# x laid out transposed as well and the mean folded into Wq, in a cross-attention + int8 FFN kernel on one core

## The reference, cut to what matters

```
x = x + xattn(layernorm(x), ctx, ctx, Wq, Wo)          # x: 4 x 2048 x 512, ctx: 4 x 77 x 512
    Q, K, V = split16(q @ Wq.T), split16(k @ Wq.T), split16(v @ Wq.T)
    attn    = softmax(Q K^T / sqrt(32)); out = (attn V) @ Wo.T
x = x + ffn(layernorm(x))                              # int8 fake quantisation of activations and weights
    h = quant(silu(xq @ wg.T) * (xq @ wu.T)); out = h @ quant(w_down).T       # inner size 1408
layernorm(x) = (x - mean) / sqrt(var + 1e-5)           # over the last axis, no scale or shift
```

## Time and profile before

| | |
|---|---|
| median of 3 runs | 1194.74 us (1194.72 to 1195.95) |
| profiled execution | 1194.37 us, of which the span is 1192.5 us |
| PE busy | 1125.9 us, 94% of the span |
| DVE, ACT, POOL busy | 861.6, 661.0 and 160.0 us |
| mean granted TensorE clock | 0.981 of 2.4 GHz |
| slots 3 to 24 (from 81.97 to 295.27 us) | 213.3 us for 22 slots |
| slots 25 to 55 (to 599.28 us) | 304.0 us for 31 slots |
| slots 56 to 65 (to 677.32 us) | 78.0 us for 10 slots |

### The profile page before, as it was taken

The page is one execution under the profiler, slowest core; times in us unless marked ns, Lnnn a source line. Parts: engine busy times, 40 slices in busy tenths (PEclk is TensorE's granted clock), DMA queues, the critical chain, the costliest instruction groups (busy, mean ns, idle before and its releaser), DMA issues. The chain is left out here.

```text
span 1192.5 us, 17719 instructions
## 1 busy us (share of the span) xinstructions
PE 1125.9 (94%) x6357; PEld 645.7 (54%) x6386; DVE 861.6 (72%) x1616; ACT 661.0 (55%) x819; POOL 160.0 (13%) x124
## 2 busy tenths in 40 slices
PE   5789999999999999999999969999999999799898
PEld 4555666666666666666665534444444444344333
DVE  5457888888878787877665667787777777575564
ACT  3347666556565655565544436657566663854450
POOL 1300000020000100000000000000000000357578
PEclk9989999999999999999999979999999999899999
DMA  5125555455343434332114626766767512899977
GB/s 182 36 59 141 125 133 132 130 130 135 103 130 108 125 109 124 109 106 65 63 54 151 216 79 229 257 219 236 237 223 251 175 46 89 333 412 419 422 279 257
DMA packets 130096, 203.51 MB, mean 171 GB/s; under 512 B 58080, under 2 KB 66912, under 8 KB 124128
## 3 DMA queue, kind: packets, MB, share of 16 engines
q1 hardware_dynamic: 130016, 202.46, 52.2%
HBM read 117.75 MB, written 72.48 MB: 160 GB/s over the span
## 5 line engine op out<-in xcount | busy, mean ns | idle before, releaser
L655 PE MATMUL a_Q<-a_xnT,wq 128*128 128x512 f32 x768 | 196.6, 405 | 3.1 <-DVE a_xnT L587 2.4
L1003 POOL TENSOR_TENSOR c_y<-x,c_y 128x512 f32<-128x512 f32 x64 | 114.3, 1816 | 554.7 <-DVE c_y L1037 544.1
L889 DVE SCALAR_TENSOR_TENSOR h<-e_U,x_gus,e_sg 128x512 f32<-128x512 f32 x176 | 131.9, 749 | 72.5 <-PE e_U L929 46.7
L834 ACT ACTIVATE e_sg<-e_G,x_gus 128x512 f32<-128x512 f32 x176 | 119.0, 685 | 117.0 <-PE e_G L925 117.0
L925 PE MATMUL e_G<-e_cT,gu 128*128 128x512 bf16 x689 | 179.3, 380 | 2.3 <-ACT e_cT L848 1.5
L929 PE MATMUL e_U<-e_cT,gu 128*128 128x512 bf16 x690 | 179.7, 380 | 0.7
L691 PE MATMUL a_O<-a_wo,a_aT 128*128 128x512 f32 x720 | 177.1, 395 | 0.0
L1075 PE MATMUL c_Y<-dn,gu 128*128 128x512 bf16 x704 | 158.4, 388 | 15.3 <-DVE gu L1030 15.3
L655 PEld LDWEIGHTS a_Q<-a_xnT,wq 128*128 128x128 f32 x768 | 142.2, 191 | 55.9 <-issue 26.4
L691 PEld LDWEIGHTS a_O<-a_wo,a_aT 128*128 128x128 f32 x720 | 133.4, 189 | 28.1 <-issue 2.5
L453 ACT ACTIVATE a_pr<-a_S 77x2048 f32<-77x2048 f32 x64 | 120.2, 1879 | 41.3 <-PE a_S L644 41.3
(11 more groups left out here) (134 smaller groups left out, 1354.2 us busy)
## 6 DMA issues: line engine op xcount, KB each, us to landing
x<-x_d SPq DMA_DIRECT2D x32, 1024.0 KB, 7.3
h_d<-h SPq DMA_DIRECT2D x24, 1024.0 KB, 4.1
h<-h_d SPq DMA_DIRECT2D x11, 1536.0 KB, 18.4
xa<-in_x SPq DMA_DIRECT2D x64, 256.0 KB, 3.1
a_xr<-in_x SPq DMA_DIRECT2D x64, 256.0 KB, 2.6
x_d<-a_xr SPq DMA_DIRECT2D x64, 256.0 KB, 2.0
out<-c_y SPq DMA_DIRECT2D x15, 1024.0 KB, 11.6
h<-h_d SPq DMA_DIRECT2D x11, 1280.0 KB, 15.2
```

The lines of the kernel that those rows point to most:

```text
L655: mm = nc.tensor.matmul(Q[:], wq[:, wp, j, P * n.g:P * (n.g + 1)], xnT[:, n.par, xp, j], start=(ins == 0), stop=(ins == 3 * KT - 1))
L834: nc.scalar.activation(sg[:, s], G[:, t % GU], ACT.Silu, scale=gus[:, t:t + 1]).then_inc(silued, 1)
L889: nc.vector.scalar_tensor_tensor(out=h[:, place(u, p), t], in0=U[:, t % GU], scalar=gus[:, IT + t:IT + t + 1], in1=sg[:, s], op0=ALU.mult, ...
L1003: nc.gpsimd.tensor_tensor(y[:, p, t], x1[:, p, t], y[:, p, t], ALU.add).then_inc(added, 1)
```

## The change

- x also comes in transposed (`xT_all`, laid out by the caller). Tiles of it go through a ring `xt32` of four and are split into `xT` directly. The normalisation of `xa`, its four transposes a slot and the copy out of PSUM are gone. A second copy of x still comes in (`xs`, ring of two) for the layernorm statistics.
- The mean is taken out of Wq instead: PE sums Wq with an all-ones matrix, DVE subtracts (`wc32`), and `wq` is the split of that. K and V use the plain split `wr`.
- 1/sqrt(var) is applied to q afterwards: once a block (k % 4 is 3) four transposes turn `rs` into `A`, DVE copies it as `rsb`, and DVE multiplies every q by it (`q32`), from which ACT and POOL make high and low part.
- The low parts of `aT`, `xT` and `qT` are made by POOL, not by DVE.
- In a slot PE now does scores, q, turns, output projection, maximum scores, sums and A V. The maximum scores are of item k+4, whose q was made in the same slot. Scores are of item k-1, one slot less behind.
- On DVE `measure` now stands at the end of the slot, behind the maximum. `w_c` on ACT still stands at the end of its slot, and POOL's cast at the start of POOL's.
- SP has one more load a slot (256 KB), and the first weight rows wait for the split of Wo, which has its own buffer.

```diff
 @block.gpsimd
 for k in SLOTS:
     if (w := weight(k - W_FIRST - 1)) and w.coded:
         pool.wait_ge(w_coded, w.code + 1)
...
+    if k == -5:
+        pool.wait_ge(mask_in, 16)
+        pool.wait_ge(k_hi, GROUPS)
+        spread_k(0)
+    if (n := at(k, -2)):
+        pool.wait_ge(aT_h, n.n + 1)
+        nc.gpsimd.tensor_tensor(aT[:, n.par, 1, n.g], att[:], aT[:, n.par, 0, n.g].bitcast(F32),
+                                ALU.subtract).then_inc(aT_l, 1)
+    if (n := at(k, 8)):
+        pool.wait_ge(xT_h, n.n + 1)
+        nc.gpsimd.tensor_tensor(xT[:, n.par, 1, n.g], xt32[:, n.n % RINGX], xT[:, n.par, 0, n.g].bitcast(F32),
+                                ALU.subtract).then_inc(xT_l, 1)
+    if (n := at(k, 4)):
+        pool.wait_ge(qT_h, n.n + 1)
+        nc.gpsimd.tensor_tensor(qT[:, n.ring, 1], q32[:], qT[:, n.ring, 0].bitcast(F32), ALU.subtract).then_inc(qT_l, 1)
 @block.scalar
+    if (n := at(k, 8)):
+        act.wait_ge(xt_in[n.n % RINGX], 16 * (n.n // RINGX + 1))
+        after(act, q_done, GROUPS * (n.block - 1))
+        nc.scalar.activation(xT[:, n.par, 0, n.g], xt32[:, n.n % RINGX], ACT.Copy).then_inc(xT_h, 1)
...
+    if (n := at(k, 4)):
+        after(act, scored, n.n - RINGQ + 1)
+        act.wait_ge(q_scaled, n.n + 1)
+        nc.scalar.activation(qT[:, n.ring, 0], q32[:], ACT.Copy).then_inc(qT_h, 1)
 @block.vector
     if done:
         dve.wait_ge(rcp_rdy, done.n + 1)
         dve.wait_ge(valued, done.n + 1)
         after(dve, aT_l, done.n)
         nc.vector.tensor_tensor(att[:], A[:], rcp[:], ALU.mult).then_inc(att_rdy, 1)
...
-    if (w := weight(k - W_FIRST - 1)) and w.measured:
-        measure(w)
-    if k % 4 == 1 and (n := at(k, -1)):
+    if k % 4 == 0 and (n := at(k, 0)):
         dve.wait_ge(m_turned, n.block + 1)
         nc.vector.tensor_copy(mT[:], A[:]).then_inc(mT_rdy, 1)
-    if (n := at(k, 3)):
+    if (n := at(k, 4)):
+        dve.wait_ge(q_done, n.n + 1)
+        after(dve, qT_l, n.n)
+        dve.wait_ge(rsb_rdy, n.block + 1)
+        nc.vector.tensor_tensor(q32[:], Q[:], rsb[:], ALU.mult).then_inc(q_scaled, 1)
+    if k % 4 == 3 and (n := at(k, 5)):
+        dve.wait_ge(r_turned, n.block + 1)
+        after(dve, q_scaled, n.n)
+        nc.vector.tensor_copy(rsb[:], A[:]).then_inc(rsb_rdy, 1)
...
+    if (n := at(k, 4)):
         dve.wait_ge(m_scored, n.n + 1)
...
                                 AX.X, ALU.max).then_inc(maxed, 1)
+    if (w := weight(k - W_FIRST - 1)) and w.measured:
+        measure(w)
 @block.tensor
+    mm = nc.tensor.matmul(A[:], allones[:], wq32[:, j], start=(j == 0), stop=(j == KT - 1))
...
-    now = at(k, -2)
+    now = at(k, -1)
...
     if (n := at(k, 4)):
-        turned = n.n + 4 if k > 7 else n.n - n.g + 4
-        after(pe, xnT_h, turned)
-        after(pe, xnT_l, turned)
-        after(pe, qT_l, n.n)
+        pe.wait_ge(xT_l, GROUPS * (n.block + 1))
+        after(pe, q_scaled, n.n)
...
+    if k % 4 == 3 and (n := at(k, 5)):
+        pe.wait_ge(rs_rdy, n.block + 1)
+        after(pe, att_rdy, k - 1)
+        for t in range(TT):
+            mm = nc.tensor.transpose(A[:, P * t:P * (t + 1)], rs[:, t:t + 1].to_broadcast([P, P]), id32[:])
+        mm.then_inc(r_turned, 1)
...
-    if (n := at(k, 8)):
-        for j in range(KT):
-            mm = nc.tensor.transpose(bank[:, P * j:P * (j + 1)], xa[:, n.n % RINGX, P * j:P * (j + 1)], id32[:])
```

More of the change, by code:

```diff
@@ L247, in attend @@
         DN = ps("a_DN", [P, 512])
-        xa_in = [sem(f"a_xa_in{r}") for r in range(RINGX)]
+        xs_in = [sem(f"a_xs_in{r}") for r in range(RINGS)]
+        xt_in = [sem(f"a_xt_in{r}") for r in range(RINGX)]
         xr_in = [sem(f"a_xr_in{g}") for g in range(TT)]
@@ L429, in _ @@
                 for k in SLOTS:
[L430 to L436, removed]
                     if k == -1:
                         act.wait_ge(w_in, 16)
-                        nc.scalar.activation(wo[:, 0], xr[:], ACT.Copy).then_inc(w_split, 1)
-                    done = at(k, -3)
+                        nc.scalar.activation(wo[:, 0], wo32[:], ACT.Copy).then_inc(w_split, 1)
+                    done = at(k, -2)
                     if done:
@@ new lines, in _ @@
+                    if k % 4 == 3 and (n := at(k, 5)):
+                        dve.wait_ge(r_turned, n.block + 1)
+                        after(dve, q_scaled, n.n)
+                        nc.vector.tensor_copy(rsb[:], A[:]).then_inc(rsb_rdy, 1)
+                    if new and new.g == 3:
+                        after(dve, r_turned, new.block)
+                        dve.wait_ge(r0_rdy, new.block + 1)
+                        own.step(nc.vector.tensor_tensor(rt[:], r0[:], r0[:], ALU.mult))
+                        own.step(nc.vector.tensor_tensor(rt[:], rt[:], ve[:], ALU.mult))
+                        own.step(nc.vector.tensor_scalar(rt[:], rt[:], -0.5, 1.5, ALU.mult, ALU.add))
+                        nc.vector.tensor_tensor(rs[:], rt[:], r0[:], ALU.mult).then_inc(rs_rdy, 1)
@@ new lines, in _ @@
+                    if (n := at(k, -6)):
+                        dve.wait_ge(projected, n.n + 1)
+                        dve.wait_ge(xr_in[n.g], 16 * (n.block + 1))
+                        t = xr[:, n.g]
+                        nc.vector.memset(hold[:], 0.0)
+                        nc.vector.tensor_tensor_reduce(t, projection(n), t, 1.0, -3.0e38, ALU.add, ALU.max,
+                                                       mv1[:, n.g, 2:3]).then_inc(x1_rdy, 1)
+                    if (n := at(k, 4)):
@@ L667, in _ @@
                         mm.then_inc(m_turned, 1)
-                    if (n := at(k, 3)):
+                    if (n := at(k, -6)):
+                        pe.wait_ge(w_split, 2)
+                        after(pe, aT_l, n.n - n.g + 4)
+                        if n.block < BLOCKS - 1:
+                            after(pe, x1_rdy, n.n)
+                        ins = 0
+                        for ap, wp in ((0, 0), (0, 1), (1, 0)):
+                            for j in range(KT):
+                                mm = nc.tensor.matmul(projection(n), aT[:, n.par, ap, j, P * n.g:P * (n.g + 1)], wo[:, wp, j],
+                                                      start=(ins == 0), stop=(ins == 3 * KT - 1))
+                                ins += 1
+                        mm.then_inc(projected, 1)
+                    if (n := at(k, 4)):
                         after(pe, exped, n.n - 4)
```

274 lines of the change are left out of this document (127 added, 147 removed).

## The result

The new kernel takes 1244.1 us (median, 1238.0 to 1245.4), the kernel before took 1195.35 us on the same chip: a ratio of 1.040, 95% interval 1.036 to 1.043. It is slower, as forecast, by 49 us where the forecast had 31, and 2 us beyond the end of the range.

What follows compares the result with a forecast made beforehand. PE's order was taken to bound the attention stage, DVE not far below. Slots 3 to 24 +54, slots 25 to 55 -13.8, start +2.7 and end -12 gave +31 on 1194.4: 1225 us, range 1200 to 1242.

Steps and rivals of the forecast that it cites:

- The loop: Slots 3 to 24: measuring behind the maximum makes DVE, ACT and POOL wait in a chain, +54 us with clock losses.
- The plain period: Slots 7 to 22 apart from every fourth: 11.04 us from maximum to maximum, with PE idle about 2 us.
- The fourth slot: Slots with k % 4 of 0: q waits for all four xT low parts, maximum at M+13.44 us.
- the clock term: Slots 3 to 24: PE's lower clock behind idle gaps, 6 x 1.5 = 9 us plus 3 in plain slots.
- The port: DVE's two-input Newton step instructions might wait for POOL's subtractions: 0 in the sum, up to +6 us in the range.
- -13.8: Slots 25 to 55: PE alone binds and loses transposes, 9.36 us a slot for 9.81, saving 13.8 us.
- Start and end: First q to slot 3: uncovered wait from q to qT, +2.7 us (-2 to +8); slots 56 on: -12 us.
- the two faster rivals: Alternatives for slots 3 to 24: POOL outside the wait chain (1186 us, chance 0.10) or no chain (1158 us, 0.04).
- The signs: Slots 3 to 24: PE idle before maximum scores, 11.6 to 12.2 us a slot; from slot 25 no gaps, 9.4.
- POOL is not in the loop: Slots 3 to 24: only DVE and ACT bind, period 10.4 us, +15 in place of +54, total 1186; chance 0.10.
- The loop does not close: Slots 3 to 24: ACT's late row is absorbed, PE binds throughout, about 200 us there, total 1158; chance 0.04.
- worse: Slots 3 to 24: low PE clock and POOL's port, 12 and 15.5 us slots, total 1243 to 1249; chance 0.17.

Runs made afterwards that it cites:

- experiment 3: New kernel plus thrown-away PE matmuls in slots 3 to 24, 10 ahead of q every fourth slot, 7 ahead of maximum scores otherwise: 1228.6 us, ratio 1.030.
- Experiment 4: New kernel with the Newton step (four tiny DVE instructions each fourth slot) moved behind the maximum: 1239.0 us, ratio 1.040.
- experiment 2: New kernel with POOL's cast of the quantised row moved behind its three subtractions: 1204.4 us, ratio 1.010.
- experiments 8 and 9: New kernel with measuring at its old place and Newton step behind the maximum, 1179.4 us; the same plus six thrown-away matmuls in slots 1 to 5, 1174.9 us.

## Why the prediction was right in kind and short in size

**The loop.** Right, step by step. L509 is followed at once by Ln, `att` waits for POOL's low part (22 times, 2.9 us each), PE idles ahead of the maximum scores and every fourth slot ahead of q, with the releasers named. The plain period was to be 11.04 and is 10.76 in slots 9, 13, 17 and 21, 0.3 below. The fourth slot was to be 13.44 without the clock and is 13.3 in experiment 3, which has a full clock. All 22 slots were to take 255.2 without clock losses. They take 258.7 in experiment 3, with 5.7 of it made by the extra matmuls, so about 253.

**The step that failed** is the size of the clock term: "In the plain slots PE then has the 2 us of slack to pay with, so I add 3 in all", with "6 x 1.5 = 9" ahead of it. Together 12 us. Experiment 3 measured 19.5 between the traces and 15.5 between the medians, and without the 5.7 that its own matmuls cost, the estimate is 21 to 25. Both halves were too small. Slots 4, 16, 20 and 24 are 2.5 to 2.7 us longer than in experiment 3, not 1.5: the 1.5 was read from one q of 4.58 us in the earlier trace rows, and slot 16 has 5.49. That q stands behind a slot that had run slow itself, and its clock is 0.53 over q and the turn. Slots 8 and 12 did cost the 1.5 (14.8 against 13.3); q in slot 12 has 4.50. And the slack of a plain slot pays for a slow q only if what follows on the loop is not PE's. Behind the 2.20 us idle in slot 14, A V, the scores and q of slot 15 all ran slow, 1.59, 1.57 and 4.75 us where 1.04, 0.92 and 3.0 are usual, and slot 15 took 0.6 longer than in experiment 3, and about 1.6 longer than it would at a full clock without the extra matmuls.

**The port.** The sum took 0 and the range 6. Experiment 4 measured 4.9 us in slots 25 to 55. That is the larger part of why -13.8 became -7.4; without the port it is 291.75 - 304.01 = -12.3. The other 1.5 is in the turns, which cost 0.46 to 0.52 where I took the 0.38 of the turn before. For slots 3 to 24 the prediction looked at the wrong instruction: the Newton step was not caught there, but L575 was, for 0.69 us more than usual in each of slots 10, 14, 18 and 22, together some 3 us. The prediction watched the step's two-input instructions alone. In the rows the one-input L602 and L575 and the copy L583 were caught as well. The Trainium skill (SBUF — State Buffer, section "Who interferes with whom") has these too: a VectorE copy or tensor_scalar in a two-port mode is kept out while GpSimd holds the shared port, and waits for its whole instruction. The trace agrees in the rows of slot 26, where 1.22 and 1.29 us stand for 0.17, and in all 26 overlaps. Slots 34 and 46 are no exception, since nothing overlapped there. Which mode DVE was in, no row shows.

**Start and end.** +4.3 for +2.7, within its bounds, by two errors that partly cancel. The first q started at 26.57, 2.1 us earlier than before, and the seven slots from it to slot 3 took 59.7, not 56. In slots 1 and 2 PE idles 1.5 to 1.6 us ahead of the maximum scores and q falls to the low clock once (4.36 us at 69.44). The end, -10.7 for -12.

**The sum.** Predicted 54 - 13.8 + 2.7 - 12 = +31, measured 65.0 - 7.4 + 4.3 - 10.7 = +51. Of the 20 us between, 11.0 are in slots 3 to 24. All of them are the clock's, by the estimate above: the loop at a full clock took about 253 for 255.2, the port's 3 us in it, and the clock about 25 for 12 in these two traces. 6.4 are in slots 25 to 55, 1.6 in the start and 1.3 at the end. By the medians there are 49 us in place of 51, and the trace of the new kernel is the slowest of its four executions.

**Range and signs.** The low end of the range is worked out, the high end is not: the port's 6 and a start of +8 in place of +2.7 lead from 1225 to 1236, and 1242 has no term behind it. The chances don't add up quite either: the two faster rivals have 0.14 together where "faster" has 0.12. The signs came as described, but larger: 12.6 us a slot in slots 3 to 24 where 11.6 to 12.2 stood, and from slot 25 on 9.57 with gaps where 9.4 without gaps stood.

**The rivals.** *POOL is not in the loop* fell: with POOL taken out, experiment 2 is 40 us faster than the new kernel. It came to 1204 where the rival had 1186. The rival's 10.4 a slot is right for the slots where DVE and ACT alone bind (10.36). 9 of the 18 us are in the other slots up to 24, and 9 in slots 25 to 55, mostly because the port catches the Newton step in all eight slots there. *The loop does not close* fell too. No kernel reached its 1158: with the order of measuring undone, 1176 is measured, and 1169.5 with the Newton step and the first slots mended. The *worse* case (1243 to 1249) gave the right total for partly right reasons. The clock came, and so did the port, but the plain slots were at 10.8 to 12.3 with two of three slowed, and not all at 12. That its total fits within 1 us is luck.

## What to carry to other kernels

When an instruction is moved to the end of one engine's slot, ask which engine's next slot begins with a wait for it: the loop over the engines is then as long as the sum of its parts, and an engine with little work (POOL, busy for 108 of the 278 us) can hold three others. Price an idle gap on PE twice, once for itself and once for the matmuls behind it at the low clock, and expect that loss to carry into the next gap. With a second engine on the shared port, put tiny DVE instructions where that engine rests, and look for that place in each stretch by itself. Before reading a gain off two traces, see which of its kernel's executions each one is: here one was the fastest and the other the slowest.

## What the runs showed of the hardware that was not expected

- A DVE instruction on 128x4 took up to 1.29 us beside a POOL subtraction of 1.29, against 0.17 alone. Copy, tensor_scalar and two-input forms were all caught, each time that they began while the subtraction ran (260 of 260 in ten traces), and ended with it. Of the DVE instructions on 128x512 in the same stretch, q32 (L591), which has one input in PSUM, took 0.68 to 0.69 beside a subtraction as without one.
- 172 thrown-away matmuls made a stretch of 278 us shorter by 19.5 between two traces, at a granted clock of 1.00 for 0.86 (15.5 us between the medians of the two kernels). In the first slots, from 67 to 120 us, the clock rose from 0.84 to 0.94 by 30 of them (experiments 8 and 9).
- Idle gaps of 1.38 us ahead of the maximum scores (219.17) were not followed by a slow q, and those of 2.20 (230.79) were. In slot 1, q at 69.44 was slow behind an idle 2.13 at 65.80 and another 1.54 at 68.14, and in slot 2, q at 79.01 was not, behind 1.53 at 75.34. So the length of one gap did not decide it in these rows.
- After 3.55 us idle q took 4.50 in slot 12 and 5.49 in slot 16, with the same work.
